# The last heads of a first attention in pairs of tiles, and the experts' routing in two halves under them

## The chip, the cores and the metric

The kernel runs on one core of one Trainium2 chip. The metric is the device time of one execution in microseconds. Five engines work side by side, each through its own program in a fixed order: PE (TensorE), DVE (VectorE), ACT (ScalarE), POOL (GpSimd) and SP (SyncE, which here only starts transfers). They wait for each other through semaphores.

## The reference

The input is eight batches (`NB`) of 512 tokens with 256 features: 32 tiles (`NN`) of 128 tokens. Four blocks follow each other, with two residual additions:

```python
x = x + _L0_attn_ref(_L0_cond_ref(x, ...), ...)      # causal attention, 16 heads of 64; then attention over the heads of a token
x = x + _L0_ffn_ref(_L0_cond2_ref(x, ...), ...)      # 8 experts, top 2, plus a shared expert; then attention and 8 experts, top 1
```

The change touches the end of the first line and the start of the second. The end of the first line works on each token by itself, over its 16 heads of 16 features:

```python
q, k, v = ...                                        # (B, T, 16 heads, 16), k and v through a latent of 64
att = softmax(einsum('bthd,btgd->bthg', q, k) / 4)   # 16 x 16 scores in each token
out = einsum('bthg,btgd->bthd', att, v) @ Wout + bout
```

The start of the second line routes each token to two of eight experts, and adds a shared expert:

```python
scores = softmax((x @ wt.T + repeat(g @ wg.T)) / 2)
topk_w, topk_idx = top_k(scores, 2)
y = sum of the two experts' outputs, weighted + (leaky(x @ sw_gate) * (x @ sw_up)) @ sw_down
```

## The kernel before, in words

The program has five parts with a fence between each two (`meet`): SP waits until all transfers of the part have landed, and every engine waits until all five have arrived. Part 0 is the first attention with the heads of batches 0 to 6, part 1 the "tail" (the heads of batch 7, and the routing of the others), part 2 the experts in pairs of slots, part 3 the second attention, part 4 the last experts. The order of each part is a list of steps written out by hand, and each engine walks the same list and does its share of each step. So a step's place in the list sets its place on all five engines.

**Heads of batch 7.** Four tiles `t` of 128 tokens. `q2` and `kv2` project on PE (DVE and ACT copy out). `hs` and `hv` come in quarters `u`: a product of 128x1024 elements (`product`, on POOL or DVE, for batch 7 half of them on each), then a reduction on DVE (`product_sum`) in the next step. The products lie in a ring of three cells. `hs_soft`, `hs_sum`, `hv_end` are small DVE and ACT operations; `turn_o` and `x1` project back on PE, POOL adds the bias to the residual (loaded by SP in step `turn_o`) and DVE adds both into the tile of `e_x1`, which SP also writes to `x1_scratch` (`x_scratch` in the profile) in step `x1`.

**Routing.** For each batch `r_turn` transposes 512 tokens on PE in two halves (ACT copies each), `r_score` computes the logits, ACT copies them, `r_back` transposes them back. These wait for each other in turn. The tokens are routed in two lots: batches 0 to 6 (`LOT[0]`, 28 tiles) and batch 7 (`LOT[1]`, 4 tiles). For a lot, `r_lgc`, `r_soft`, `r_rank`, `r_cnt`, `r_oh` compute the softmax and each token's two experts on DVE, and `count` gives each token its slot: two matmuls on PE and a running sum on DVE. `scatter n` writes tile n's rows to their two slots in `xe_scratch` with two indirect transfers, issued by POOL. `slots` finds the expert of each pair of slots. Part 2 then gathers the slots from `xe_scratch` with indirect transfers from POOL (`fetch`).

**Shared expert.** Steps `shared i`, 0 to 17: gate and up projections (PE), two DVE operations one step later, and in each second step from 3 on the down projection of an earlier batch, which ACT copies and SP writes to `y_scratch`.

**The order before.** The list of part 1 takes a step of the heads and a step of the rest in turn (`order_tail`): the seven batches' routing stands beside tiles 0 and 1, the first scatters and shared steps beside tiles 2 and 3, the remaining scatters behind, and last `e_load`, in which ACT starts 24 loads of expert weights. Behind the fence, part 2 begins with batch 7's routing, shared steps 14 to 17, the last eight scatters and `slots`, then the experts. PE's transposes and logits of the routing use one bank (`rR`) in part 1.

Of the kernel before, what the change touches and what calls it, by code (L numbers as in the profile page):

```python
# [242 lines left out]

def head_steps(b):
    yield [("turn_h", b, 0)]
    yield [("turn_h", b, 1)]
    yield [("lat", b)]

    def front(t):
        yield [("q2", b, t)]  # L250
        yield [("kv2", b, t)]

    def middle(t):
        for u in range(4):
            yield [("hs", b, t, u)]
        yield [("hs_soft", b, t)]
        yield [("hs_sum", b, t)]
        for u in range(4):
            yield [("hv", b, t, u)]
        yield [("hv_end", b, t)]  # L260

    def back(t):
        yield [("turn_o", b, t)]
        yield []
        yield [("x1", b, t)]

    late = 3 if b < NB - 1 else 2
    for i in range(NT + late):
# [14 lines left out]
def order_one():  # L283
# [49 lines left out]
    return out, [y for part in head_steps(NB - 1) for y in part]  # L333
# [637 lines left out]
def order_early():


    out = [("r_init",)]
    for b in range(NB - 1):
        out += [("r_turn", b), ("r_score", b), ("r_back", b)]
    out += routes(0)
    for n in range(*LOT[0]):
        out.append(("scatter", n))
        if n % 2:  # L980
            out.append(("shared", n // 2))
    return out


def order_tail(heads_left):

    early, out, due = order_early(), [("e_weights",)], -6.0
    for x in heads_left:
        out.append(x)
        due += 1.0  # L990
        while early and due >= 1.0:
            due -= 1.0
            out.append(early.pop(0))
    return out + early + [("e_load",)]


def order_two():
    b = NB - 1
    out = [("r_last",), ("r_turn", b), ("r_score", b), ("r_back", b)]
    i = 2 * (NB - 1)  # L1000
    for x in routes(1):
        out.append(x)
        if i < 2 * NB + 2 and x[0] in ("r_soft", "r_rank", "r_cnt", "count"):
            out.append(("shared", i))
            i += 1
    out += [("scatter", n) for n in range(*LOT[1])] + [("slots",), ("mha_load",)]
    out += [("expert", j) for j in range(4)] + [("gate", 0), ("gate", 1), ("places", 0), ("places", 1)]
    return out + [("expert", j) for j in range(4, NS_E // 2 + 3)]


def setup_two(k, nc, ins):
    sb, low = Arena(nc, k.split, k.hi), Arena(nc, k.base + 17 * 1024, k.split)
    k.tail = order_tail(k.tail1)
# [43 lines left out]
    k.rR, k.rL, k.rG = Ring(k.bank[0:1]), Ring(k.bank[2:3]), Ring([k.bank[1], k.bank[3]])  # L1057
# [44 lines left out]


def tensor_two(k, pe, w, order):
    did, ident = k.c.did, k.ident
    for step, *key in order:
# [4 lines left out]
        elif step == "r_last":  # L1111
            k.rR.cells, k.rR.n = [k.bank[0], k.bank[4]], 0
            k.rD.cells, k.rD.n = [k.bank[7], k.bank[0]], 0
# [27 lines left out]
        elif step == "count":  # L1141
# [3 lines left out]
            mr, mt = [k.rG.take((x, g), at("c_exc", g, 0), at("c_exc", g, 1)) for x in ("rank", "total")]  # L1145
# [206 lines left out]
def count(k, dv, w, g):  # L1352
# [4 lines left out]
    mr, mt = [k.rG.of((x, g)).ap[:, 0:n * E8].rearrange("p (t x) -> p t x", x=E8) for x in ("rank", "total")]  # L1357
# [1179 lines left out]
```

## Time and profile before

| | |
|---|---|
| median of 3 runs | 2675.94 us (2673.14 to 2695.26) |
| profiled execution | 2696.61 us, span 2694.7 us |
| PE busy | 2216.2 us, 82% of the span |
| DVE, ACT, POOL busy | 1473.1, 1181.2, 976.3 us (55%, 44%, 36%) |
| mean granted TensorE clock | 0.901 of full speed |

The shares are means over the whole span. The stretch of interest is a tenth of it, from about 1158 us (heads of batch 7 begin) to 1425.7 us (PE's first transposes for the experts), and has to be read by itself: the timeline of each engine there gives, for each group of instructions, when it began, how long it took, and in brackets how long the engine stood before it and which engine and tile ended the wait. "issue" stands for a wait for nothing that the profile shows.

### The profile page before, as it was taken

The page shows a single profiled execution, that of the slowest core. Times are in us where ns is not written, and L with a number is a line of the kernel's source. Part 1 is how long each engine was busy: PE and PEld are TensorE (multiplying, and loading weights), DVE is VectorE, ACT ScalarE, POOL GpSimd, SP SyncE. Part 2 cuts the span into 40 slices and gives each one's busy share as a digit, 9 for nine tenths or more (in the row PEclk, how much of TensorE's full clock was granted, in tenths as well). Part 3 has the DMA queues.
Part 4 walks back from the last instruction along what each step waited for, and adds up shares of the span by engine and source line. Part 5 has one row for each costly group of instructions (what it writes and reads, how often), then busy time and mean ns, then how long its engine had stood idle before and what let it go on. Part 6 is the DMA issues. An engine that isn't in the chain of part 4 may idle for free.

```text
span 2694.7 us, 33460 instructions
## 1 busy us (share of the span) xinstructions
PE 2216.2 (82%) x11652; PEld 1170.7 (43%) x11652; DVE 1473.1 (55%) x3091; ACT 1181.2 (44%) x2748; POOL 976.3 (36%) x751
## 2 busy tenths in 40 slices
PE   3989898989898989855857949899999988844996
PEld 1545555545455545522436823233333322222764
DVE  2336767676767676746523436666666660231336
ACT  1756666666666666611112411455555443220221
POOL 0105647474738374822725421112221110213005
PEclk9999999999999999967978967999999995576998
DMA  6032212112100000020344431111111004152214
GB/s 223 10 108 74 75 64 83 64 67 84 51 22 5 14 5 13 8 77 22 109 128 138 149 94 40 32 44 42 56 42 36 26 11 128 54 160 82 63 58 129
DMA packets 160464, 181.18 MB, mean 67 GB/s; under 512 B 18666, under 2 KB 144874, under 8 KB 160043
## 3 DMA queue, kind: packets, MB, share of 16 engines
q1 hardware_dynamic: 78402, 73.43, 8.9%
q10 hardware_dynamic: 69224, 70.99, 7.9%
q0 software_dynamic: 12672, 34.62, 4.1%
q8 instruction: 95, 1.56, 0.2%
q14 instruction: 71, 0.57, 0.1%
HBM read 88.03 MB, written 86.77 MB: 65 GB/s over the span
## 4 chain that ended last, share of the span: by engine, by line
PE 61%; DVE 12%; POOL 10%; ACT 8%; issue 4%; ACTq 3%; DMA 2%; SPq 0%; DVEq 0%; POOLq 0%
PE ps L1789 11%; POOL prod L793 6%; ACT m_pt L1917 6%; PE ps L513 4%; PE ps L527 4%; PE ps L1800 3%; PE ps L538 3%; PE ps L552 3%; DVE pb L676 3%; PE ps L562 3%; PE ps L2109 3%; PE ps L2117 3%; PE ps L1755 2%; DVE sc L805 2%; PE ps L1195 2%
## 5 line engine op out<-in xcount | busy, mean ns | idle before, releaser
L1917 ACT ACTIVATE m_pt<-ps 128x1024 f32<-128x1024 f32 x256 | 262.2, 1024 | 347.1 <-PE ps L1789 347.1
L1854 DVE TENSOR_REDUCE m_mx<-ps 128x2 f32<-128x1024 f32 x256 | 312.5, 1224 | 183.9 <-PE ps L1773 182.9
L676 DVE CUSTOM_DVE_ANT_0 pb<-ps,bias,snl 128x128 f32<-128x128 f32 (+3 forms) x512 | 260.8, 547 | 257.0 <-PE ps L527 254.4
L793 POOL TENSOR_TENSOR prod<-qs,kvs 128x1024 f32<-128x1024 f32 x120 | 284.3, 2395 | 230.6 <-issue 130.7
L1789 PE MATMUL ps<-m_q,m_k 32*128 32x512 f32 x1024 | 318.5, 701 | 56.6 <-ACT m_pt L1917 48.9
L793 POOL TENSOR_TENSOR prod<-sc,kvs 128x1024 f32<-128x1024 f32 x120 | 278.7, 2348 | 110.0 <-ACT sc L911 101.2
L873 ACT ACTIVATE pb<-pb,mst 128x129 f32<-128x129 f32 (+3 forms) x512 | 283.5, 559 | 69.3 <-DVE mst L676 67.3
L1773 PE MATMUL ps<-m_k,m_q 32*128 32x512 f32 x1024 | 293.2, 673 | 5.2 <-DVE m_mx L1854 5.2
L884 ACT ACTIVATE ptb<-ps 128x512 f32<-128x512 f32 (+2 forms) x384 | 181.6, 491 | 151.2 <-PE ps L538 148.2
L538 PE MATMUL ps<-ident,pb 128*128 128x128 f32 x1280 | 188.7, 284 | 63.5 <-ACT rsb L860 62.7
L538 PEld LDWEIGHTS ps<-ident,pb 128*128 128x128 f32 x1280 | 143.0, 144 | 125.3 <-ACT rsb L860 68.2
L527 PE MATMUL ps<-kz,qT 64*128 64x128 f32 (+3 forms) x1024 | 186.2, 442 | 0.0
L805 DVE TENSOR_REDUCE sc<-prod 128x64 f32<-128x1024 f32 x128 | 152.5, 1211 | 46.1 <-POOL prod L793 45.6
L1789 PEld LDWEIGHTS ps<-m_q,m_k 32*128 32x128 f32 x1024 | 83.3, 198 | 205.2 <-ACT m_pt L1917 184.2
L1944 POOL DMA_INDIRECT m_yg<-ye_scratch,e_pos x64 | 63.2, 987 | 289.8 <-DVE m_x L1842 253.5
L552 PE MATMUL ps<-ptb,vt 128*64 128x512 f32 (+3 forms) x1024 | 158.3, 452 | 7.9 <-DVE xr L750 7.9
L805 DVE TENSOR_REDUCE ob<-prod 128x64 f32<-128x1024 f32 x128 | 152.6, 1210 | 18.7 <-POOL prod L793 18.6
L1800 PE MATMUL ps<-m_pt,m_va 128*32 128x512 f32 x1024 | 150.6, 664 | 0.0
L513 PE MATMUL ps<-xnT,w_wq 128*128 128x512 f32 x256 | 134.4, 651 | 0.9
L1954 POOL TENSOR_TENSOR m_lnrs<-m_lnve,mhalf 128x1 f32<-128x1 f32 x32 | 17.7, 552 | 290.6 <-DVE m_lnve L761 290.6
L562 PE MATMUL ps<-w_wo,oTT 128*128 128x256 f32 x512 | 122.5, 383 | 0.1
L552 PEld LDWEIGHTS ps<-ptb,vt 128*64 128x64 f32 x1024 | 71.0, 141 | 92.1 <-issue 81.5
(310 smaller groups left out, 3764.1 us busy)
## 6 DMA issues: line engine op xcount, KB each, us to landing
xe_scratch<-zt ACTq DMA_DIRECT2D x32, 1024.0 KB, 4.5
ye_scratch<-e_ys SPq DMA_DIRECT2D x36, 256.0 KB, 2.1
hw_w<-in_w ACTq DMA_DIRECT2D x16, 512.0 KB, 3.6
xs_scratch<-zt ACTq DMA_DIRECT2D x1, 4992.0 KB, 16.3
h_xs<-xs_scratch SPq DMA_DIRECT2D x39, 128.0 KB, 2.2
ys_scratch<-h_ys SPq DMA_DIRECT2D x39, 128.0 KB, 1.7
xin<-in_x SPq DMA_DIRECT2D x8, 512.0 KB, 3.6
bias<-in_fside ACTq DMA_DIRECT2D x8, 512.0 KB, 11.8
```

Of the source, the lines that this page charges most:

```text
L513: i = pe.matmul(m.ap, k.wq[:, c, p * P:(p + 1) * P], xn.ap[:, c, :], start=(c == 0), stop=(c == 1))
L527: pe.matmul(ms[j].ap[:, 0:n], q.ap[DH * j:DH * j + DH, t * P:(t + 1) * P], kz.ap[DH * j:DH * j + DH, 0:n], start=False, stop=True, tile_po ...
L538: i = pe.transpose(m.ap[:, j * P:(j + 1) * P], pb[:, SEG[t] + kt * P:SEG[t] + (kt + 1) * P], ident[:, :])
L552: i = pe.matmul(m.ap[DH * j:DH * j + DH, kt * P:S], v.ap[:, kt, :], pt.ap[:, KEYCOL[kt]:KEYCOL[kt + 1]], start=(kt == 0), stop=(kt == NT - ...
L676: dv.tensor_tensor_reduce(pb.ap[:, j, SEG[t]:SEG[t] + n], rS.of(("S", b, p, t, j)).ap[:, 0:n], k.bias[:, h, CAUSAL[t]:CAUSAL[t + 1]], -1.0 ...
L793: e.tensor_tensor(out, one, two, ALU.mult).then_inc(*k.c.did(*product_done(step, b, t, u)))
L805: dv.tensor_reduce(heads(dst.ap[:, :])[:, 4 * u:4 * u + 4, :], src, AX, ALU.add).then_inc(*k.c.did(step + "_r", b, t, u))
L873: ac.activation(part, part, ACT.Exp, bias=ms[:, 0, j, t:t + 1], scale=-1.0, accum_out=ms[:, 1, j, t:t + 1]).then_inc(*did("exp", b, p, t, j))
L1773: x = pe.matmul(m.ap[:, i, :], band(q.ap, j)[:, t * P:(t + 1) * P], band(kk.ap, j), start=True, stop=True, tile_position=(32 * j, 0))
L1789: x = pe.matmul(m.ap[:, i, :], band(kk.ap, j)[:, kt * P:(kt + 1) * P], band(q.ap, j), start=True, stop=True, tile_position=(32 * j, 0))
L1854: dv.tensor_reduce(x.ap[:, t, 64 * half:64 * half + 64].rearrange("p (i r) -> p i r", i=2)[:, :, 16], k.qS.of((b, g, t, half)).ap, AX, ALU ...
L1917: ac.activation(p.ap[:, 2 * half:2 * half + 2, :], k.qE.of((b, g, kt, half)).ap, ACT.Exp).then_inc(*did("m_exp", b, g, kt, half))
```

## The change

`order_tail` is written anew. The heads of batch 7 go two tiles at a time: tiles 0 and 1 step by step together (`one`), with the `r_turn`, `r_score`, `r_back` of batches 0 to 6 between, two of these steps after each step of the heads; then tiles 2 and 3 together (`two`), with lot 0's routing, counting and shared steps 0 to 5 between. Then come `e_load`, the end of tiles 2 and 3 with shared steps 6 to 8, the 28 scatters of lot 0, batch 7's routing with shared steps 9 to 13, the four scatters of lot 1, `slots`, and shared steps 14 to 17. All of this stands ahead of the fence; part 2 begins with `mha_load` (nine loads on ACT) and the experts. The weights are loaded by SP in place of ACT. The routing's ring has three banks in place of one, and the counting's two matmuls get banks of their own (`rC`). `head_front`, `head_middle` and `head_back` hold the steps of a tile as the functions inside `head_steps` did.

```diff
+def last_heads():
+
+
+    b = NB - 1
+    start = [[("turn_h", b, 0)], [("turn_h", b, 1)], [("lat", b)]]
+    start += [x for t in range(2) for x in head_front(b, t)]
+    one = list(weave((head_middle(b, 0), 11), (head_middle(b, 1), 11), (head_front(b, 2), 2))) + list(head_front(b, 3))
+    two = list(weave((head_middle(b, 2), 11), (head_middle(b, 3), 11), (head_back(b, 0), 3), (head_back(b, 1), 3)))
+    return start, one, two, list(weave((head_back(b, 2), 3), (head_back(b, 3), 3)))
...
-def order_early():
-
-
-    out = [("r_init",)]
-    for b in range(NB - 1):
-        out += [("r_turn", b), ("r_score", b), ("r_back", b)]
-    out += routes(0)
-    for n in range(*LOT[0]):
-        out.append(("scatter", n))
-        if n % 2:
-            out.append(("shared", n // 2))
-    return out
-
-
-def order_tail(heads_left):
-
-    early, out, due = order_early(), [("e_weights",)], -6.0
-    for x in heads_left:
-        out.append(x)
-        due += 1.0
-        while early and due >= 1.0:
-            due -= 1.0
-            out.append(early.pop(0))
-    return out + early + [("e_load",)]
-
-
-def order_two():
-    b = NB - 1
-    out = [("r_last",), ("r_turn", b), ("r_score", b), ("r_back", b)]
-    i = 2 * (NB - 1)
-    for x in routes(1):
-        out.append(x)
-        if i < 2 * NB + 2 and x[0] in ("r_soft", "r_rank", "r_cnt", "count"):
+def order_tail():
+
+
+    start, one, two, end = last_heads()
+    turns = [("r_init",)] + [(x, b) for b in range(NB - 1) for x in ("r_turn", "r_score", "r_back")]
+    out = [("e_weights",)] + [x for part in start for x in part]
+    for part in one:
+        out += part + turns[:2]
+        turns = turns[2:]
+    out += turns
+    chain, i = routes(0), 0
+    for n, part in enumerate(two):
+        out += part + chain[:1]
+        chain = chain[1:]
+        if n % 2 == 0:
             out.append(("shared", i))
             i += 1
-    out += [("scatter", n) for n in range(*LOT[1])] + [("slots",), ("mha_load",)]
-    out += [("expert", j) for j in range(4)] + [("gate", 0), ("gate", 1), ("places", 0), ("places", 1)]
+    out += chain + [("e_load",)]
+    for part in end:
+        out += part + [("shared", i)]
+        i += 1
+    out += [("scatter", n) for n in range(*LOT[0])]
+    b = NB - 1
+    for x in [("r_turn", b), ("r_score", b), ("r_back", b)] + routes(1):
+        out.append(x)
+        if x[0] in ("r_turn", "r_back", "r_soft", "r_rank", "r_cnt"):
+            out.append(("shared", i))
+            i += 1
+    return out + [("scatter", n) for n in range(*LOT[1])] + [("slots",)] + [("shared", j) for j in range(i, 2 * NB + 2)]
+
+
+def order_two():
+    out = [("mha_load",)] + [("expert", j) for j in range(4)] + [("gate", 0), ("gate", 1), ("places", 0), ("places", 1)]
     return out + [("expert", j) for j in range(4, NS_E // 2 + 3)]
...
-    k.rR, k.rL, k.rG = Ring(k.bank[0:1]), Ring(k.bank[2:3]), Ring([k.bank[1], k.bank[3]])
+    k.rR, k.rL, k.rG = Ring([k.bank[0], k.bank[5], k.bank[6]]), Ring(k.bank[2:3]), Ring([k.bank[1], k.bank[3]])
+    k.rC = Ring([k.bank[2], k.bank[0]])
...
+        if step == "e_load":
+            for x in range(E8):
+                g4 = k.gu[:, x, :].rearrange("p (c k m) -> p c k m", c=2, k=2)
+                sp.dma_start(g4[:, :, 0, :], ins["moe_gate"][x].rearrange("(c p) m -> p c m", p=P)).then_inc(*did("d_gu", 2 * x))
+                sp.dma_start(g4[:, :, 1, :], ins["moe_up"][x].rearrange("(c p) m -> p c m", p=P)).then_inc(*did("d_gu", 2 * x + 1))
+                sp.dma_start(k.dn[:, x, :], ins["moe_down"][x]).then_inc(*did("d_dn", x))
...
-            mr, mt = [k.rG.take((x, g), at("c_exc", g, 0), at("c_exc", g, 1)) for x in ("rank", "total")]
+            mr, mt = [k.rC.take((x, g), at("c_exc", g, 0), at("c_exc", g, 1)) for x in ("rank", "total")]
...
-                load("gu", 2 * x, g4[:, :, 0, :], ins["moe_gate"][x].rearrange("(c p) m -> p c m", p=P))
-                load("gu", 2 * x + 1, g4[:, :, 1, :], ins["moe_up"][x].rearrange("(c p) m -> p c m", p=P))
-                load("dn", x, k.dn[:, x, :], ins["moe_down"][x])
```

POOL, from the heads' products of batch 7 to the first gather (`prod` the products, `xr` the residual, `xe_scratch` the scatters, `e_xs` the gathers). Before:

```order
L793 TENSOR_TENSOR prod<-sc_116,kvs_114 128x1024 x2
L793 TENSOR_TENSOR prod<-qs_109,kvs_112 128x1024
L1584 DMA xe_scratch<-e_x_144,e_sposi 32768x256 x4
L952 TENSOR_TENSOR xr_125<-xr_125,w_bout 128x256
L793 TENSOR_TENSOR prod<-qs_109,kvs_112 128x1024
L1584 DMA xe_scratch<-e_x_144,e_sposi 32768x256 x6
...
L1584 DMA xe_scratch<-e_x_144,e_sposi 32768x256 x4
L952 TENSOR_TENSOR xr_125<-xr_125,w_bout 128x256
L1584 DMA xe_scratch<-e_x_144,e_sposi 32768x256 x28
L1593 DMA e_xs_182<-xe_scratch,e_gix 128x256 x2
```

Now:

```order
L805 TENSOR_TENSOR prod<-sc_115,kvs_112 128x1024
L805 TENSOR_TENSOR prod<-sc_116,kvs_113 128x1024
L805 TENSOR_TENSOR prod<-sc_115,kvs_112 128x1024
L805 TENSOR_TENSOR prod<-sc_116,kvs_113 128x1024
L964 TENSOR_TENSOR xr_124<-xr_124,w_bout 128x256
L964 TENSOR_TENSOR xr_125<-xr_125,w_bout 128x256
L1591 DMA xe_scratch<-e_x_144,e_sposi 32768x256 x64
L1600 DMA e_xs_182<-xe_scratch,e_gix 128x256 x2
```

The scatters stood between the products of tiles 2 and 3; now all 64 stand behind the last product and the last residual of the heads.

SP, from the residual loads of tiles 0 and 1 to the experts' first write (`xr` the residual, `x_scratch` the heads' output, `e_y` the shared expert's). The 24 loads of the weights stand in the middle, of which the first three are shown. Before:

```order
L465 DMA x_scratch<-e_x_144 128x256
L461 DMA xr_125<-in_x 128x256
L465 DMA x_scratch<-e_x_144 128x256
L1094 DMA y_scratch<-e_y_179 128x4x256
L461 DMA xr_124<-in_x 128x256
L1094 DMA y_scratch<-e_y_180 128x4x256
L1094 DMA y_scratch<-e_y_179 128x4x256
L465 DMA x_scratch<-e_x_144 128x256
L461 DMA xr_125<-in_x 128x256
L465 DMA x_scratch<-e_x_144 128x256
```

Now:

```order
L1109 DMA y_scratch<-e_y_179 128x4x256
L477 DMA x_scratch<-e_x_144 128x256 x2
L1109 DMA y_scratch<-e_y_180 128x4x256
L1101 DMA ew_gu<-in_moe_gate 128x2x128
L1102 DMA ew_gu<-in_moe_up 128x2x128
L1103 DMA ew_dn<-in_moe_down 128x256
...
L1103 DMA ew_dn<-in_moe_down 128x256
L473 DMA xr_124<-in_x 128x256
L473 DMA xr_125<-in_x 128x256
L1109 DMA y_scratch<-e_y_179 128x4x256
L477 DMA x_scratch<-e_x_144 128x256 x2
```

The residual loads of tiles 2 and 3 stand behind the 24 weight loads, which before were ACT's.

PE, from the first projections of batch 7's heads on (`hT` the input, `latT` the latent, `e_x` the rows that are routed). Before:

```order
L599 MATMUL ps<-w_awq,hT 128x256 x2
L605 MATMUL ps<-w_wup,latT 128x512
L1110 MATMUL ps<-ew_cT,ew_wg 8x8
L1120 MATMUL ps<-ident,e_x_144 128x128 x8
L1127 MATMUL ps<-e_xT,ew_wt 8x512 x2
L1139 MATMUL ps<-ident,e_lgT_198 128x8 x4
L599 MATMUL ps<-w_awq,hT 128x256 x2
L1120 MATMUL ps<-ident,e_x_144 128x128 x8
```

Now:

```order
L611 MATMUL ps<-w_awq,hT 128x256 x2
L617 MATMUL ps<-w_wup,latT 128x512
L611 MATMUL ps<-w_awq,hT 128x256 x2
L617 MATMUL ps<-w_wup,latT 128x512
L1125 MATMUL ps<-ew_cT,ew_wg 8x8
L1132 MATMUL ps<-ident,e_x_144 128x128 x8
L1139 MATMUL ps<-e_xT,ew_wt 8x512 x2
...
L1151 MATMUL ps<-ident,e_lgT_198 128x8 x4
L611 MATMUL ps<-w_awq,hT 128x256 x2
L1132 MATMUL ps<-ident,e_x_144 128x128 x8
```

Tile 1's two projections stand ahead of the routing, and tile 2's first behind the third batch of it.

## Rows read from the trace of the kernel before

**Rows 1.** Windows of core 0: stretch, length, busy PE, PEld, DVE, ACT, POOL, clock, DMA.

```profile
1158.00:1237.50 79.50, 47.43 (x144) 17.64 (x142) 37.13 (x41) 18.34 (x35) 21.22 (x10) 0.71 0.18 59
1237.50:1364.50 127.00, 88.27 (x236) 46.87 (x236) 72.57 (x95) 17.85 (x34) 79.63 (x67) 0.85 0.25 86
1380.60:1425.70 45.10, 22.85 (x69) 12.66 (x69) 15.83 (x49) 5.69 (x10) 10.89 (x12) 0.69 0.30 99
```

**Rows 2.** Timeline of POOL: start, length, instruction, wait before it and its releaser.

```profile
1264.11 1.21 POOL L1584 DMA_INDIRECT xe_scratch<-e_x,e_sposi  x1 [24.31 <-DVE e_sposi L1388]
...
1321.00 1.73 POOL L1584 DMA_INDIRECT xe_scratch<-e_x,e_sposi  x1 [0.30 <-issue]
...
1343.73 0.97 POOL L1584 DMA_INDIRECT xe_scratch<-e_x,e_sposi  x1 [2.12 <-issue]
...
1360.21 0.96 POOL L1584 DMA_INDIRECT xe_scratch<-e_x,e_sposi  x1 [0.31 <-issue]
...
1406.28 0.98 POOL L1584 DMA_INDIRECT xe_scratch<-e_x,e_sposi  x1 [45.12 <-DVE e_sposi L1388]
...
1415.16 0.96 POOL L1584 DMA_INDIRECT xe_scratch<-e_x,e_sposi  x1 [0.30 <-issue]
...
1421.60 0.99 POOL L1593 DMA_INDIRECT e_xs<-xe_scratch,e_gix  x1 [5.48 <-DMA xe_scratch<-e_x,e_sposi]
```

**Rows 3.** Timeline of PE, the same columns.

```profile
1179.26 0.63 PE L1120 MATMUL ps<-ident,e_x 128*128 128x128 f32 x4 [0.95 <-ACT e_cs L1518]
...
1222.58 1.88 PE L1127 MATMUL ps<-e_xT,ew_wt 128*8 128x512 f32 x4 [0.69 <-ACT e_xT L1523]
...
1380.64 1.97 PE L1120 MATMUL ps<-ident,e_x 128*128 128x128 f32 x8 [16.23 <-SPq L2441]
...
1425.68 1.12 PE L1184 MATMUL ps<-ident,e_xs 128*128 128x128 f32 x4 [19.61 <-DMA e_xs<-xe_scratch,e_gix]
```

**Rows 4.** Groups of PE by line, 1156 to 1420.5: busy, mean ns, idle before.

```profile
L1127 PE MATMUL ps<-e_xT,ew_wt 128*8 128x512 f32 x32 | 25.4, 943 | 5.5 <-ACT e_xT L1523 5.5
...
L1120 PE MATMUL ps<-ident,e_x 128*128 128x128 f32 x64 | 12.7, 337 | 23.6 <-SPq L2441 16.2 <-ACT e_xT L1523 6.4 <-ACT e_cs L1518 1.0
...
L599 PE MATMUL ps<-w_awq,hT 128*128 128x256 f32 x16 | 5.4, 466 | 0.0
...
L1139 PE MATMUL ps<-ident,e_lgT 8*128 8x8 f32 x32 | 3.6, 218 | 5.1 <-ACT e_lgT L1528 5.1
```

**Rows 5.** Groups of DVE by line, 1156 to 1380: busy, mean ns, idle before.

```profile
L805 DVE TENSOR_REDUCE ob<-prod 128x64 f32<-128x1024 f32 x16 | 19.3, 1212 | 14.0 <-POOL prod L793 13.9
...
L793 DVE TENSOR_TENSOR prod<-qs,kvs 128x1024 f32<-128x1024 f32 x8 | 12.4, 1550 | 8.2 <-ACT kvs L905 8.2
...
L793 DVE TENSOR_TENSOR prod<-sc,kvs 128x1024 f32<-128x1024 f32 x8 | 10.7, 1336 | 0.0
...
L1330 DVE TENSOR_TENSOR e_aT<-ps,e_lk 128x512 f32<-128x512 f32 x13 | 9.0, 692 | 6.7 <-PE ps L1170 6.4
```

**Rows 6.** Timeline of DVE.

```profile
1183.30 2.20 DVE L793 TENSOR_TENSOR prod<-qs,kvs 128x1024 f32<-128x1024 f32 x1
...
1233.27 0.39 DVE L1292 COPY e_lg<-ps 128x224 f32<-128x224 f32 x1 [3.22 <-PE ps L1139]
...
1251.78 0.27 DVE L1485 TENSOR_SCALAR e_oh<-e_gt 128x224 f32<-128x224 f32 x1
...
1255.49 0.62 DVE L1360 COPY e_cum<-ps 128x448 f32<-128x448 f32 x1 [2.31 <-PE ps L1149]
```

**Rows 7.** Timeline of ACT and its queue (ACTq).

```profile
1364.45 0.39 ACTq L1492 DMA_DIRECT2D ew_gu<-in_moe_gate  x1
...
1411.65 0.51 ACTq L1492 DMA_DIRECT2D m_x<-y_scratch  x1
```

**Rows 8.** Chain that ended last, in order of time: start, length, what.

```profile
1376.85 3.47 DMA ew_dn<-in_moe_down
```

**Rows 9.** Transfers by line, 1290 to 1430: issuer, count, KB, us to landing.

```profile
xr<-in_x SPq DMA_DIRECT2D x2, 128.0 KB, 2.8
```

More of the change, by code:

```diff
@@ L241, in pre_steps, with head_front, head_middle, head_back @@
     yield [("vals", b)]
+def head_front(b, t):
+    yield [("q2", b, t)]
+    yield [("kv2", b, t)]
+def head_middle(b, t):
+    for u in range(4):
+        yield [("hs", b, t, u)]
+    yield [("hs_soft", b, t)]
+    yield [("hs_sum", b, t)]
+    for u in range(4):
+        yield [("hv", b, t, u)]
+    yield [("hv_end", b, t)]
+def head_back(b, t):
+    yield [("turn_o", b, t)]
+    yield []
+    yield [("x1", b, t)]
 def head_steps(b):
@@ L247, in head_steps @@
     yield [("lat", b)]
[L249 to L268, printed above, removed]
+    for i in range(NT + 3):
         parts = []
-        if i >= late:
-            parts.append((back(i - late), 3))
+        if i >= 3:
+            parts.append((head_back(b, i - 3), 3))
         if i < NT:
-            parts.append((front(i), 2))
+            parts.append((head_front(b, i), 2))
         if 1 <= i <= NT:
-            parts.append((middle(i - 1), 11))
+            parts.append((head_middle(b, i - 1), 11))
         yield from weave(*parts)
+def last_heads():
[5 more added lines that the diff above has]
+    return start, one, two, list(weave((head_back(b, 2), 3), (head_back(b, 3), 3)))
 CLEARS = 32
@@ L332, in order_one @@
     out += [y for part in hd[0] for y in part]
-    return out, [y for part in head_steps(NB - 1) for y in part]
+    return out, [y for stage in last_heads() for part in stage for y in part]
 def setup_one(k, nc, ins):
@@ L1012, in setup_two @@
     sb, low = Arena(nc, k.split, k.hi), Arena(nc, k.base + 17 * 1024, k.split)
-    k.tail = order_tail(k.tail1)
+    k.tail = order_tail()
     k.exc, k.inc = [None, None], [None, None]
@@ L1086, in sync_two @@
 def sync_two(k, sp, w, order):
-    did = k.c.did
+    did, ins = k.c.did, k.ins
     for step, *key in order:
-        if step == "shared":
+        if step == "e_load":
[4 more added lines that the diff above has]
+                sp.dma_start(k.dn[:, x, :], ins["moe_down"][x]).then_inc(*did("d_dn", x))
+        elif step == "shared":
             i = key[0]
@@ L1110, in tensor_two @@
             pe.matmul(m.ap[0:E8, 0:NB], k.wg[:, :], k.cT[:, :], start=True, stop=True).then_inc(*did("e_cs", 0))
-        elif step == "r_last":
-            k.rR.cells, k.rR.n = [k.bank[0], k.bank[4]], 0
-            k.rD.cells, k.rD.n = [k.bank[7], k.bank[0]], 0
         elif step == "r_turn":
@@ L1172, in tensor_two @@
         elif step == "mha_load":
+            k.rR.cells, k.rR.n = [k.bank[0], k.bank[4]], 0
             k.rD.cells, k.rD.n = [k.bank[7], k.bank[2]], 0
@@ L1356, in count @@
     n = 2 * (n1 - n0)
-    mr, mt = [k.rG.of((x, g)).ap[:, 0:n * E8].rearrange("p (t x) -> p t x", x=E8) for x in ("rank", "total")]
+    mr, mt = [k.rC.of((x, g)).ap[:, 0:n * E8].rearrange("p (t x) -> p t x", x=E8) for x in ("rank", "total")]
     w.wait_ge(at("c_mm", g, 1))
```

3 lines of the change are left out of this document (removed).

## The prediction

> **What bounds the kernel now.** I read the stretches of time first, then the timeline of each engine in the one stretch that the change touches. The first attention ends near 1158 us, the paired experts' first transposes start at 1425.68 [rows 3]. The change moves work only between these two marks; before and behind them the programs are the same. In that stretch no engine is full: PE, DVE and POOL are each busy for half of the time or less from 1158 to 1237.5, and POOL alone comes over 60% from 1237.5 to 1364.5 [rows 1]. So what counts is the chain. On POOL it reads like this [rows 2]: the first scatter at 1264.11 waited for the slot numbers from DVE; 56 scatters then run to 1361.2, mixed with POOL's products for the last two tiles of heads; POOL idles 45 us until 1406.28, because batch 7's routing stands behind the fence; 8 more scatters, a wait for their landing, the first gather at 1421.60, and PE 4.1 us later. A run of scatters with nothing between costs 1.27 us each (1343.73 to 1360.21 is 13 steps). Ahead of the fence ACT issues 24 weight loads from 1364.45 [rows 7] on; the last is issued at 1376.85 (to about 1377.3) and lands at 1380.32 [rows 8], and PE resumes at 1380.64 [rows 3], 0.3 us later.
>
> **What goes.** The fence now stands behind all 64 scatters, so the hole of 45 us on POOL goes, and so do the 16 us in which nothing computes while ACT issues the weights. In return no scatter may start until the last head tile is out, since all of them stand behind POOL's last two additions of the residual. The question is when that is.
>
> **First half of the heads.** Its length is set by the routing chain of seven batches on PE and ACT, not by the heads. The first routing transpose is at 1179.26 [rows 3]; tile 1's two projections and their copies now come first, about 1.3 us (bounds 0.5 and 2.5), so 1180.6. A batch is eight transposes (12.7/8 = 1.59), a wait for ACT (5.5/8 = 0.69), the scores (25.4/8 = 3.18), a wait (5.1/8 = 0.64) and the transposes back (3.6/8 = 0.45) [rows 4]: 6.55, and 45.9 for seven. Before it took 54 (1179.26 to 1233.27, when DVE copies the logits [rows 6]), mainly since one bank made the second transposes wait for the first copy; now there are three banks. Three more projections stand in the chain, 1.35 each (5.4/4) or less: 3.5 in all. Half one ends at 1230. DVE needs some 34.5 us for two tiles (below), has one wait for tile 2's projection, which stands behind the third batch, and is done by about 1221: hidden under the chain, by 9 us.
>
> **Second half.** Here DVE is the bound. All its work in the first two stretches is 37.13 + 72.57 = 109.7 us [rows 1]. Of that, 13 shared steps take twice 9.0 = 18.0 [rows 5] (two operations each, of one size), or 1.38 a step. Routing of seven batches is 14.4: from 1233.27 to 1252.05 [rows 6] less five head operations between, 4.4 (three of 1.2 and two of 0.4). The counting runs from 1255.49 to 1263.8 [rows 6], 8.3. The counting ends where POOL's first scatter begins, at 1264.11, less 0.3. The rest, 69, is four tiles of heads, so 34.5 for two. Half two holds two tiles (34.5), routing (14.4), counting (8.3) and four shared steps (5.5): 62.7. PE's two counting matmuls took 3.4 us between the one-hots and the first copy [rows 6]; 2.7 us of other DVE work now stands there, so 0.7 of wait. Tiles 0 and 1 are out at 1230 + 63.4, about 1294.
>
> **Then SyncE.** It writes two tiles, and then issues the 24 weight loads ahead of the residual rows of tiles 2 and 3: 28 issues. ACT needed 1364.45 to 1377.3 for its 24, 12.9 us or 0.54 each [rows 7, 8]; I take the same for SyncE, 15.0 (bounds 12 and 17). A residual load takes 2.8 to land [rows 9], the last weights took 3.5 from the start of their issue [rows 8]; beside them I take 3.3. POOL's addition is 0.7. This is a wait the change creates: POOL has no product left from about 1291 on and stands until 1294 + 15.0 + 3.3 + 0.7 = 1313.0. The weights' issue is still not hidden; it has moved from ahead of the fence to ahead of the scatters.
>
> **Scatters.** 64 at 1.27 are 81.2. The 56 of before have two pauses in which nothing is waited for that the profile shows, one of 2.12 [rows 2] and one like it; less the usual 0.3 each, about 3.7. End at 1397.9. Under them lie batch 7's routing and shared steps 8 to 17 on PE, DVE and ACT. In the stretch from 1237.5 to 1364.5 PE was busy for 88.27 us [rows 1], with fourteen shared steps and some head work, so a step costs at most 6.3 and ten at most 63; batch 7's routing adds a batch's 6.55. That is 70, inside 85: hidden, but it would be the next bound.
>
> **Behind the scatters.** From the last scatter's end to the first gather 5.2 us (1416.4 to 1421.60), now with a fence of 0.3 between, and 4.1 from there to PE [rows 2, 3]: PE at 1407.5. What is new is that ACT issues its nine attention loads before the first copy; they took about 6 us, the last of them at 1411.65 [rows 7]; the first stood right behind ACT's last copy, so ACT is free about 0.8 after PE's first transposes, and the gathers share the DMA engines with these loads. I take 1.5 (bounds 0.5 and 5). That makes 1409.0, 16.7 before 1425.7. Phase two has about ten hand-overs between engines that each work in a fixed order, and I have costed one at 0.7; the others I bound by 0 and 12 us and take 3, nearer to nothing, because most of the partners are over half idle. **Sum: 14 us gained.**
>
> The expert stage itself stays: PE sets its pace, and it starts from a rest either way.
>
> **Rivals.** *The lock.* Two tiles at once put DVE's products beside POOL's more often. A DVE product beside one of POOL took 2.20 us [rows 6], while the means are 1.55 and 1.34 [rows 5]. Were all eight in half two at 2.20, that is 4 x 0.65 + 4 x 0.86 = 6 us more; with the hand-overs at their upper bound (9 more than I took) the gain is gone: 2676. It decides when DVE's half two passes 80 us. For it: three product cells serve two tiles. Against: the more numerous reductions show no such growth, 1.21 each in the mean [rows 5]. The Trainium skill, SBUF — State Buffer, section Who interferes with whom, says that a DVE instruction with two SBUF inputs and a GpSimd one that reads SBUF exclude each other for a whole instruction; by that rule each of the eight waits for a POOL product, and the trace agrees in the slowed row.
>
> *A quicker chain.* The scores took 1.88 us in one batch [rows 3] against a mean of 3.18: PE ran at the higher of its two levels there. Half one packs PE more densely (three banks), and if all seven batches ran so, 9 us more would be gained: 23, or 2653. Against: the granted clock over this stretch is 0.71 [rows 1], and the chain still waits at every step.
>
> *Slower.* 64 scatters now stand in one row, and anything that slows their issue counts 64 times. Beside a DVE product a scatter took 1.73 us [rows 2] in place of 0.96; were that the rule for all that DVE does now beside the scatters (shared steps, batch 7's routing), 64 x 0.77 = 49 us are added, and the result is 35 us slower, 2711. It decides from 0.65 us per scatter for a slowdown of 1%. Against it: the products are over by then, and 14 scatters in a row beside DVE's shared steps kept 1.27 [rows 2], as did the eight beside the counting and `slots` (1406.28 to 1415.16 is seven steps of 1.27). The Trainium skill, SBUF — State Buffer, section SBUF: two separate sides, warns that descriptors of a GpSimd DMA can't be written while DVE runs a mode with two ports; by that, DVE's copies beside the scatters could do it too.
>
> *The change doesn't do it.* If the weights' issue and the residual's late load eat what the fence gives, little is left; this is in the sum already (about 20 us of standing POOL), and an issue of 17 us with 5 of landing and 5 behind the scatters leaves 7: inside my range.
>
> **Numbers.** The profiled execution took 2696.61 (span 2694.7); the median of the runs is 2675.94 and they spread from 2673.14 to 2695.26. The sum of -14 is made against the profile's own time, which becomes 2682.6; I apply the same to the median: **2662**. Chances: this forecast, 6 to 20 us gained, 0.62; the quicker chain 0.14; gain gone (between 6 gained and 10 lost) 0.19; slower by more than that 0.05. A measurement of this kernel can tell about 1%, 27 us, from no change. Over that on the quick side lies only the outer part of the quicker chain, with every other bound at its best: 0.08. Slower by over 1%: 0.04. Within: 0.88. The range: 17 us to the quick side and 18 to the slow one takes in the bounds of the sum (issue 3, hand-overs 9, gathers 4, lock 6 against 9 of clock) and a few us of the spread of runs: 2645 to 2680.
>
> **What would show it.** In the profile after: the last transposes back of batch 6 near 1230 (if at 1222, the quicker chain); tile 1's output on DVE near 1294 to 1300 (over 1310: lock and hand-overs); POOL idle for some 20 us ahead of the first scatter, released by the DMA of the residual, and that scatter near 1313 to 1316; 64 scatters at 1.27 with two or three pauses (at over 1.9: the slow rival); first gather about 5.5 us behind them; the experts' first transposes near 1409 to 1414. I am wrong if half one waits for DVE rather than for PE's chain, if the weights take far from 13 us to issue on SyncE, or if shared steps outlast the scatters.

## The result, and the profile after

The changed kernel took 2663.61 us in the median of 20 runs (2649.49 to 2676.92), the kernel before 2680.34 in as many (2671.78 to 2700.17). The ratio is 0.9933, with a 95% interval of 0.9911 to 0.9955: 18 us less (12 to 24), which is inside 1% and inside the range forecast (2645 to 2680; 2662 was the likeliest). The profiled execution of the changed kernel has a span of 2653.1 us, 41.6 less than the one of before. Some 19 us of that difference aren't the change's, as run e5 below shows; so I compare **the part that the change touches**, from PE's transposes of `hn` (the end of the first attention, 1156.28 before and 1156.80 now) to PE's first transposes for the experts. It was 269.4 us long (to 1425.68 [rows 3]) and is 247.0 now (to 1403.85).

The stretches of the changed kernel, as in [rows 1] (length, busy time and instructions of PE, PEld, DVE, ACT and POOL, the granted clock, the DMA share, GB/s): half one, half two, POOL's wait for the residual, the scatters, the fence and first gather.

```profile
1158.00:1222.00 64.00, 36.23 (x146) 16.97 (x145) 37.07 (x40) 17.66 (x33) 22.76 (x9) 0.82 0.25 77
1222.00:1286.00 64.00, 39.70 (x95) 20.88 (x94) 62.02 (x78) 7.93 (x16) 23.05 (x9) 0.76 0.03 9
1286.00:1305.40 19.40, 16.78 (x55) 9.62 (x53) 4.35 (x8) 4.13 (x8) 1.40 (x2) 1.00 0.81 243
1305.40:1394.30 88.90, 52.21 (x156) 29.38 (x156) 24.36 (x62) 12.14 (x21) 62.19 (x64) 0.82 0.36 126
1394.30:1403.80 9.50, 0.00 (x0) 0.00 (x0) 0.00 (x0) 0.00 (x0) 5.29 (x7) 0.50 0.71 209
```

Each stretch has another limit: DVE is full in the second (62 of 64), in the third POOL stands and SyncE issues, in the fourth POOL alone sets the pace. POOL's timeline (start, length, instruction, idle time before it and what ended it) answers to [rows 2]:

```profile
1272.97 5.56 POOL L805 TENSOR_TENSOR prod<-sc,kvs 128x1024 f32<-128x1024 f32 x2 [14.05 <-DVE ob L817]
1303.89 1.40 POOL L964 TENSOR_TENSOR xr<-xr,w_bout 128x256 f32<-128x256 f32 x2 [25.36 <-DMA xr<-in_x]
1305.48 1.21 POOL L1591 DMA_INDIRECT xe_scratch<-e_x,e_sposi  x1 [0.19 <-issue]
...
1325.48 0.97 POOL L1591 DMA_INDIRECT xe_scratch<-e_x,e_sposi  x1 [2.35 <-issue]
1326.76 0.96 POOL L1591 DMA_INDIRECT xe_scratch<-e_x,e_sposi  x1 [0.30 <-issue]
...
1345.20 0.97 POOL L1591 DMA_INDIRECT xe_scratch<-e_x,e_sposi  x1 [2.11 <-issue]
...
1384.51 0.98 POOL L1591 DMA_INDIRECT xe_scratch<-e_x,e_sposi  x1 [2.11 <-issue]
...
1393.37 0.96 POOL L1591 DMA_INDIRECT xe_scratch<-e_x,e_sposi  x1 [0.30 <-issue]
1397.02 1.00 POOL L1600 DMA_INDIRECT e_xs<-xe_scratch,e_gix  x1 [2.69 <-POOLq L2448]
```

The hole of 45 us is gone. A wait of 25.4 us for the residual's rows stands ahead of the scatters in its place, and the row of scatters has four pauses (2.35, 2.11, 2.10 and 2.11 us, one after each 14). SyncE's queue shows why the rows came late: two tile writes, 24 weight loads, then the rows (22 of the loads, between the first and the last, are left out).

```profile
1285.66 0.80 SPq L477 DMA_DIRECT2D x_scratch<-e_x  x2
1287.26 0.37 SPq L1109 DMA_DIRECT2D y_scratch<-e_y  x1
1287.67 0.51 SPq L1101 DMA_DIRECT2D ew_gu<-in_moe_gate  x1
...
1299.82 0.47 SPq L1103 DMA_DIRECT2D ew_dn<-in_moe_down  x1
1300.34 0.90 SPq L473 DMA_DIRECT2D xr<-in_x  x2
```

PE in half one (the routing's chain) and at the end; [rows 3, 4] are those of before:

```profile
1205.83 1.09 PE L1132 MATMUL ps<-ident,e_x 128*128 128x128 f32 x8
1207.66 1.88 PE L1139 MATMUL ps<-e_xT,ew_wt 128*8 128x512 f32 x4 [0.74 <-ACT e_xT L1530]
1210.31 0.41 PE L1151 MATMUL ps<-ident,e_lgT 8*128 8x8 f32 x4 [0.77 <-ACT e_lgT L1535]
1210.65 1.09 PE L1132 MATMUL ps<-ident,e_x 128*128 128x128 f32 x8
...
1220.35 1.13 PE L611 MATMUL ps<-w_awq,hT 128*128 128x256 f32 x4
...
1371.78 1.99 PE L1182 MATMUL ps<-ew_sd,e_aT 128*128 128x256 f32 x8 [0.69 <-ACT e_y L1552]
1403.85 1.08 PE L1197 MATMUL ps<-ident,e_xs 128*128 128x128 f32 x4 [30.07 <-DMA e_xs<-xe_scratch,e_gix]
```

A batch of routing takes 4.82 us (1205.83 to 1210.65), 7.7 before (54 for seven [rows 3, 6]). The last shared step ends at 1373.8, 20 us ahead of the scatters: hidden, as forecast.

### The profile page after: what moved, and what is told of

The parts are those of the page before. It is cut to its first block, busy times and chain, and to the rows that moved or that the text cites. A ratio compares the mean times of both kernels' runs of the same rounds, so it can differ in the third digit from the quotient of the medians.

```text
span 2653.1 us, 33457 instructions
## 1 busy us (share of the span) xinstructions
PE 2178.8 (82%) x11652; PEld 1162.1 (44%) x11652; DVE 1475.3 (56%) x3091; ACT 1180.5 (44%) x2748; POOL 976.6 (37%) x751
## 4 chain that ended last, share of the span: by engine, by line
PE 59%; DVE 12%; POOL 10%; ACT 8%; issue 5%; ACTq 3%; DMA 2%; SPq 1%; POOLq 0%; DVEq 0%
PE ps L1796 11%; ACT m_pt L1924 6%; POOL prod L805 5%; PE ps L525 4%; PE ps L539 4%; PE ps L550 3%; PE ps L564 3%; DVE sc L817 3%; PE ps L1807 3%; DVE pb L688 3%; PE ps L574 3%; PE ps L2116 3%; PE ps L2124 3%; PE ps L1762 3%; PE ps L1208 2%
## 5 line engine op out<-in xcount | busy, mean ns | idle before, releaser
L1796 PE MATMUL ps<-m_q,m_k 32*128 32x512 f32 x1024 | 307.5, 678 | 57.5 <-ACT m_pt L1924 49.4
L550 PE MATMUL ps<-ident,pb 128*128 128x128 f32 x1280 | 188.6, 284 | 63.4 <-ACT rsb L872 62.7
L817 DVE TENSOR_REDUCE sc<-prod 128x64 f32<-128x1024 f32 x128 | 152.2, 1209 | 32.9 <-POOL prod L805 32.6
```

Of the source, the lines that this page charges most:

```text
L550: i = pe.transpose(m.ap[:, j * P:(j + 1) * P], pb[:, SEG[t] + kt * P:SEG[t] + (kt + 1) * P], ident[:, :])
L817: dv.tensor_reduce(heads(dst.ap[:, :])[:, 4 * u:4 * u + 4, :], src, AX, ALU.add).then_inc(*k.c.did(step + "_r", b, t, u))
L1796: x = pe.matmul(m.ap[:, i, :], band(kk.ap, j)[:, kt * P:(kt + 1) * P], band(q.ap, j), start=True, stop=True, tile_position=(32 * j, 0))
```

## The experiments

All are compared with the kernel before on the same chip. "Part" is the part named above, in the one profiled execution of each; it is cut at POOL's first scatter (A) and at the end of its last (B), C is what follows to the experts. The last column is the second attention behind the experts, from PE's first transposes of `m_x` to POOL's next scatter, whose code is the same in all of them. The changed kernel and e5 are the same program, and their parts differ by 4.1 us, A by 1.3, B by 1.7 and C by 1.1: differences of that size in a single profile tell nothing.

| kernel | ratio (95%) | part | A | B | C | 2nd attention, clock |
|---|---|---|---|---|---|---|
| before | 1 | 269.4 | | | | 843.3, 0.87 |
| changed | 0.9933 (0.9911 to 0.9955) | 247.0 | 148.7 | 88.9 | 9.5 | 825.2, 0.89 |
| e5, changed again | 0.9932 (0.9902 to 0.9962) | 251.1 | 150.0 | 90.5 | 10.6 | 834.6, 0.88 |
| e2, weights on SyncE only | 0.9969 (0.9943 to 0.9995) | 260.0 | | | | 839.2, 0.88 |
| e4, batch 7 behind the fence | 1.0021 (0.9994 to 1.0048) | 275.2 | 150.4 | | | 827.2, 0.89 |
| e3, 28 scatters fewer | 0.9855 (0.9819 to 0.989) | 234.1 | 150.1 | 60.3 | 23.8 | 821.4, 0.90 |
| e1, rows first | 0.9874 (0.9839 to 0.991) | 239.4 | 135.6 | 91.3 | 12.5 | 825.3, 0.89 |
| e6, and 10 scatters early | 0.9881 (0.9849 to 0.9913) | 224.7 | 121.8 | 92.9 | 10.0 | 821.7, 0.90 |
| e7, one tile at a time | 0.9965 (0.9939 to 0.9991) | 254.1 | 155.3 | 88.6 | 10.3 | 821.5, 0.90 |
| e8, one bank | 0.9987 (0.9964 to 1.0009) | 260.2 | 161.4 | 88.4 | 10.4 | 838.5, 0.88 |
| e9, chain's steps ahead | 0.994 (0.9912 to 0.9969) | 250.9 | 151.5 | 89.7 | 9.7 | 834.7, 0.88 |
| e10, loads late | 0.9918 (0.989 to 0.9947) | 244.3 | 148.5 | 89.1 | 6.8 | 833.6, 0.88 |
| e11, e6 + e9 + e10 | 0.9828 (0.9794 to 0.9862) | 224.9 | 123.7 | 94.4 | 6.8 | 845.2, 0.87 |
| e12, and 4 more early | 0.9867 (0.9829 to 0.9904) | 220.4 | 111.4 | 98.4 | 10.7 | 839.0, 0.88 |

**e5: how much of the profile's difference is the change's.**

> The changed kernel once more, unchanged, as the reference for its neighbours on this chip. If the profile's 42 us between the two kernels were the change's, its time behind the first attention (from the experts' first transposes to the end, 1249 us in the one profile and 1269 in the other) would be 1249 again and the ratio near 0.985; if that part is the spread of runs, the ratio stays near 0.993 and the part behind varies.

The ratio stayed at 0.9932, and the part behind the experts' first transposes was 1258.7 us long, neither 1249 nor 1269. The rows of the second attention (columns as above) of before, the changed kernel, e6 and e11 say what differs:

```profile
1574.30:2417.60 843.30, 730.78 (x3972) 250.55 (x3972) 453.81 (x685) 341.96 (x394) 140.35 (x182) 0.87 0.19 58
```
```profile
1554.40:2379.60 825.20, 711.96 (x3972) 245.74 (x3972) 453.85 (x685) 341.85 (x394) 140.41 (x184) 0.89 0.19 59
```
```profile
1531.50:2353.20 821.70, 707.69 (x3972) 244.71 (x3972) 453.93 (x685) 341.98 (x394) 140.33 (x183) 0.90 0.20 59
```
```profile
1536.80:2382.00 845.20, 732.03 (x3972) 250.80 (x3972) 453.92 (x685) 341.78 (x394) 140.23 (x184) 0.87 0.19 58
```

The same 3972 matmuls, and DVE and ACT busy alike to 0.2 us; only PE's busy time and the granted clock move, and the stretch with them, by 24 us. It doesn't follow the change: e11 is the slowest and has the changed kernel's order. So the part (22.4 us less in one profile, 18.3 in the other) and the ratio (18) agree, and the profiles' further 19 us are this spread.

**e2: one half of the change alone.** SyncE's step from the change, put into the kernel before, behind the last head step:

```
-    return out + early + [("e_load",)]
+    return out + [("e_load",)] + early
```

> The kernel before with one part of the change alone: SyncE, not ACT, issues the 24 weight loads, behind the last head tile's write, under the scatters. Theory (the 16 us in which ACT issues and all others stand are a cost by themselves): about 15 us less than before, 2665, which is all that the whole change gave, while POOL's hole for batch 7's routing stays at some 28 us. Rival (the issue is hidden anyway, or the loads slow the scatters): within 4 us of before.

The part is 9.4 us shorter and the ratio 8 us (1 to 15), not 15, though the ratio's interval just reaches 15: the shared steps and the landing of their last write now held the fence up, and PE resumed at 1373.69 in place of 1380.64 [rows 3]; POOL's hole was 33.6 us. In that profile PE also stood 4.65 us ahead of the last down projection for a copy of ACT's, which itself stood 5.1 us for something that the profile doesn't name. So in this profile 9 of the weights' 16 us were there to be had without the rest of the change.

**e4: the other half taken back.** The rows of the order for batch 7 (`r_turn`, `r_score`, `r_back`, `routes(1)`, its scatters) stand in `order_two` again, and with them `slots`, the last shared steps and, behind them, `mha_load`.

> The changed kernel with batch 7's routing and its 8 scatters put back behind the fence. Theory (the hole behind the fence is what the change takes away): POOL stands some 26 us between the 56 scatters and the 8, and the kernel takes about 2690, more than the kernel before. Rival (the gain comes from the quicker chain and the weights, and the hole was worth little): 2665 to 2672.

28 us longer than the changed kernel in the part (24 against e5), and as slow as before:

```profile
1388.80 0.96 POOL L1593 DMA_INDIRECT xe_scratch<-e_x,e_sposi  x1 [0.30 <-issue]
1422.21 0.97 POOL L1593 DMA_INDIRECT xe_scratch<-e_x,e_sposi  x1 [32.46 <-DVE e_sposi L1403]
```

With the order of the heads, the three banks and SyncE's loads all in place, the gain is gone. It is the hole (32.5 us here) that pays, and the late first scatter is its price.

**e3: what bounds the row.** `for u in range(2)` becomes `for u in (range(1, 2) if n < LOT[0][1] else range(2))`; so 28 rows of scatters aren't written.

> The changed kernel without 28 of the 64 scatters (the first slot's row of each token tile of batches 0 to 6 isn't written). Theory (the scatters' row sets the end, the shared steps are next, which ended on PE at 1373.8): POOL's row is 28 x 1.27 + 4 shorter, but only some 19 us show, about 2645. Rival (POOL isn't what the fence waits for): no gain. Second rival (nothing else is near): all 40 us.

B fell by 29 to 30, the part by 13 to 17. POOL's waits in that stretch (who waited for whom: us in total, times, the longest):

```profile
POOL e_xs L1600 <- SPq L2448: 16.5, 1, 16.5
POOL xe_scratch L1591 <- DVE e_sposi L1401: 11.8, 1, 11.8
```

The shared steps and batch 7's routing are next, some 13 to 17 us below the scatters, as the first theory had it.

**e1 and e6: the wait ahead of the scatters.** e1 moves `("e_load",)` behind the loop over `end`. e6 adds:

```
-    out += chain
+    out += chain + [("scatter", n) for n in range(5)]
```

> SyncE issues the residual rows of tiles 2 and 3 ahead of its 24 weight loads. Theory (POOL's 25.4 us of standing ahead of the scatters are SyncE's queue): the rows are issued about 12.6 us sooner, the first scatter comes some 20 us behind the last product in place of 32, everything behind it moves by 12 to 13 us, and the kernel takes about 2651. Rival (the shared steps or the weights' landing are the next bound at once): under 5 us gained.

> As e1, and POOL issues the first 10 scatters before its two additions for tiles 2 and 3. Theory (POOL's row sets the end): the row starts some 14 us earlier, and 12 us come on top of e1's gain. Rival (behind e1 the shared steps are the bound, as its trace shows, where the last of them ended at 1387.6, after the scatters): within 3 us of e1, with POOL idle ahead of the first gather for over 10 us.

A is 13.1 us shorter in e1 (14.4 against e5), what the queue was said to cost. In its profile only 7.6 of it reached the experts: the shared steps ended last, at 1387.7 (the scatters had ended at 1386.1). PE was at the lower clock for several of them, and PE and ACT also stood for things that the profile doesn't name: PE 4.91 us ahead of 1368.15, ACT 7.87 ahead of 1356.86. What held them isn't known. It isn't the order on PE, since e6 has the same one, and there the shared steps ended at 1367.9 and the scatters set the end. e6's rival, that nothing is left beyond e1, fell in the profiles: POOL stood 2.7 us ahead of the first gather, not over 10, and the part is 14.7 us shorter still, and 22.3 to 26.4 shorter than the changed kernel's. The whole kernel's times don't confirm the further gain: e1 is 1.3% under before and e6 1.2%, on two chips, so it stands on one profile of each. e6 shows too what a scatter costs beside DVE's products; DVE, then POOL:

```profile
1279.02 1.22 DVE L805 TENSOR_TENSOR prod<-sc,kvs 128x1024 f32<-128x1024 f32 x1
1281.29 1.22 DVE L805 TENSOR_TENSOR prod<-sc,kvs 128x1024 f32<-128x1024 f32 x1
```

```profile
1279.11 2.21 POOL L1592 DMA_INDIRECT xe_scratch<-e_x,e_sposi  x1 [0.19 <-issue]
1281.62 1.72 POOL L1592 DMA_INDIRECT xe_scratch<-e_x,e_sposi  x1 [0.31 <-issue]
1283.65 0.96 POOL L1592 DMA_INDIRECT xe_scratch<-e_x,e_sposi  x1 [0.30 <-issue]
```

**e7: what the pairs are worth.** Each half runs its tiles one behind the other, with one step of the chain behind each part (and a shared step behind each fourth, not each second); the edit of half one:

```
-    one = list(weave((head_middle(b, 0), 11), (head_middle(b, 1), 11), (head_front(b, 2), 2))) + list(head_front(b, 3))
+    one = list(weave((head_middle(b, 0), 11), (head_front(b, 2), 2))) + list(weave((head_middle(b, 1), 11), (head_front(b, 3), 2)))
```

> The changed kernel with the last heads one tile at a time inside its two halves (tile 0, then 1, with the routing's chain; tile 2, then 3, with its end), all else kept. Theory (a pair fills DVE's waits for POOL's products and ACT's exponentials): DVE reaches tile 1's output 5 to 10 us later than with pairs, and the kernel is as much slower. Rival (the pair pays for DVE and POOL standing in each other's way as much as it fills): within 3 us.

A is 5.3 us longer, the part 3.0, both against e5 on the same chip, and tile 1's output came 6.0 later (counted from `hn`), as the theory had it; but 3.0 is less than the 4.1 between the changed kernel and e5, the ratios' intervals overlap, and PE's scores took 3.8 us more in this profile at the lower clock. Two tiles at a time are no loss, and worth 5 us at most; that they are worth anything isn't shown.

**e8: what the banks are worth.** `Ring([k.bank[0], k.bank[5], k.bank[6]])` becomes `Ring(k.bank[0:1])`.

> The changed kernel with one PSUM bank for the routing's transposes and scores in place of three. Theory (the banks made the chain quick: a batch took 4.8 us in the changed kernel and 7.7 before): half one is 10 to 14 us longer, and 8 to 14 of it reach the end of the kernel. Rival (the chain is quick because PE ran at its higher clock there): a batch takes 5 to 6 us with one bank, and the kernel changes by under 5.

Tile 3's projection, which ends half one, reached DVE 77.2 us behind `hn`, in e5 66.8: 10.4 longer, and 9.1 of it reached the experts. With one bank a batch reads

```profile
1212.78 1.88 PE L1139 MATMUL ps<-e_xT,ew_wt 128*8 128x512 f32 x4 [0.69 <-ACT e_xT L1530]
1215.44 0.41 PE L1151 MATMUL ps<-ident,e_lgT 8*128 8x8 f32 x4 [0.77 <-ACT e_lgT L1535]
1215.78 0.66 PE L1132 MATMUL ps<-ident,e_x 128*128 128x128 f32 x4
1217.12 0.66 PE L1132 MATMUL ps<-ident,e_x 128*128 128x128 f32 x4 [0.69 <-ACT e_xT L1530]
1218.46 3.19 PE L1139 MATMUL ps<-e_xT,ew_wt 128*8 128x512 f32 x4 [0.69 <-ACT e_xT L1530]
```

5.7 us from scores to scores at the higher clock (4.8 with three banks), and in the next batch the scores take 3.19. So one bank adds 0.9 us of waiting a batch, 6 in all. But the stall of 5.67 us that e9 is about isn't in e8, and so PE's waits in the chain sum to 14.4 us, against 14.8 in e5. The chain is 8.5 us longer by PE's own time: it was busy for 21.5 us with the scores of the seven batches, in e5 for 13.3. Both theories had a part. Why the scores ran at the lower clock isn't settled. Fewer gaps in PE's work don't explain it: e11, with three banks and only 9.9 us of waits in the chain, had three of its seven scores at 3.2 to 3.5 us, one of them here:

```profile
1190.96 3.53 PE L1140 MATMUL ps<-e_xT,ew_wt 128*8 128x512 f32 x4 [0.74 <-ACT e_xT L1531]
```

No run holds the gaps and changes the clock alone.

**e9: the one stall in half one.** In the changed kernel ACT's exponentials stood ahead of a routing copy, and PE waited 5.67 us for it at 1198.13. `out += part + turns[:2]` becomes `out += turns[:2] + part`.

> The changed kernel with two steps of the routing's chain ahead of, not behind, each part of half one's heads. Theory (half one is the chain plus one stall of 5 us, in which ACT's exponentials stood ahead of a routing copy): the stall goes or halves, half one ends 3 to 5 us earlier, and the kernel gains as much. Rival (the stall moves to the next batch, or DVE's own work for two tiles is the bound): under 1.5 us.

No gain. The stall moved to the next batch's copies, as the rival said; ACT in e9, then PE:

```profile
1199.65 0.42 ACT L923 ACTIVATE sc<-sc 128x256 f32<-128x256 f32 x1 [2.71 <-DVE sc L744]
1199.97 1.06 ACT L1530 ACTIVATE e_xT<-ps 128x512 f32<-128x512 f32 x2
```
```profile
1201.09 3.58 PE L1139 MATMUL ps<-e_xT,ew_wt 128*8 128x512 f32 x4 [3.82 <-ACT e_xT L1530]
```

**e10, e11, e12: the loads, and all together.** e10 moves ACT's nine loads behind `("expert", 2)`; e11 is e6 with e9's and e10's edits; e12 puts scatters 0 and 1 of e11's first five behind part 7 of `two`.

> The changed kernel with ACT's nine loads for the second attention behind the paired experts' third step, not ahead of the first. Theory (the first gathers share the DMA engines with these loads: 6.8 and 7.9 us from the first gather to PE in two profiles, 4.1 before): this time is 4.1 to 4.5 us again, 3 us gained. Rival (the gathers are slow for another reason, or ACT's issues now hold up its first copies for 4.6 us): no gain.

> e6, e9 and e10 together. Theory (three separate terms of one chain): e6's time less 4 less 3, about 36 us under the changed kernel in the part from the first attention's last transposes to the experts, which is some 218 us long. Rival (the shared steps take the end over once the scatters start early enough): no better than e6 less 3.

> As e11, and four of the scatters stand ahead of POOL's last two products, in the 14 us in which POOL waited there. Theory: they start when the slots are known, 5 us ahead of the products, and shorten the row behind by as much, less 1 or 2 for scatters beside DVE's products: 3 to 4 us under e11. Rival (a scatter that is slowed holds up the product that DVE waits for): 0 or a loss.

From the first gather to PE's transposes it is 4.09 us in e10, and within 0.05 of that in e11 and e12; in all kernels with `mha_load` right behind the fence it is 6.6 to 7.9. In before, e2 and e4, where the nine loads had been issued 9 us or more ahead of the first gather, it is 4.1 too. PE in e10 (the first gather began at 1403.34):

```profile
1407.43 1.09 PE L1197 MATMUL ps<-ident,e_xs 128*128 128x128 f32 x4 [27.41 <-DMA e_xs<-xe_scratch,e_gix]
```

C fell by 2.7 (3.8 against e5), as expected. e11 is not better than e6 in the part: its C is 3.2 shorter, A and B are 3.4 longer, and e9's edit, which gains nothing, is in it. e12's scatters start 12.3 us earlier, but the row is 4 longer (POOL's last two products, 4.66 us, stand in it), and then the shared steps' last write held the fence (C is 10.7): 4.5 gained in the part, which the ratio (0.9867) doesn't bear out. Of all kernels run e11 has the lowest median, 2636.04 us, 1.7% under before (1.4 to 2.1); its interval overlaps e12's.

## Why the prediction held, step by step

The mechanism was right and the gain larger than forecast: 22 us in one profile, 18 in the other and 18 by the ratio, in place of 14. The first scatter came at 1305.5, not at 1313 to 1316, and PE at 1403.9, not at 1409 to 1414. That the forecast of 2662 lies within 2 us of 2663.61 is luck: the kernel before has a median of 2680.34 in 20 runs, 4.4 over the 2675.94 in three from which I subtracted, and that offsets the 3 to 4 us that I forecast too little.

**The limit and the exchange** were right: the hole of 45 us and the weights' 16 went, a late first scatter came. e4 shows that the hole carries the gain, e2 that of the weights' 16 us on ACT 9 could be had alone.

**Half one** was the step that was mis-sized: 1230 forecast, DVE's next projection at 1221.5, which is the mark (1222) that the quicker-chain rival had named. The batches took 4.82 in place of 6.55, mostly because the scores took 1.88, not the mean of 3.18 [rows 4]. I had argued against it from the granted clock of [rows 1] (0.71), as if it would stay; it is 0.82 now, and e8 shows that one bank brings most of the slow scores back, though not why. One stall of 5.67 us behind ACT's exponentials, 4.9 more than the usual wait there, which I didn't have, gave part back.

**Half two** was right in the sum, 63.4 forecast for DVE and 63.7 measured (1221.5 to 1285.2), but not in its terms. The heads took 32.6 us, not 34.5, since none of DVE's products was slowed: 1.21 or 1.22 each. The routing took 16.7, not 14.4, because the lock between DVE and POOL, which I had looked for in the products, fell on it:

```profile
1243.13 3.24 DVE L1490 TENSOR_TENSOR e_cmp<-e_cmp,ew_before 128x1792 f32<-128x1792 f32 x1
1246.40 2.43 DVE L1492 TENSOR_TENSOR e_cmp<-e_cmp 128x1792 f32<-128x1792 f32 x1
```

Before, the same two took 2.02 and 2.03. POOL had a product until 1244.49 and then the additions for tiles 0 and 1, which took 4.97 us (those for tiles 2 and 3 took 1.40, at 1303.89). The two errors cancel.

**SyncE's queue** was right to 1.3 us: 19.0 forecast from tile 1 to the first scatter, 20.3 measured; the 24 loads took 12.6 us, and e1 gave 13 of it back.

**The row of scatters** was 4 us short: two pauses were read from before, where one of POOL's products (behind 28 scatters) hid the third and the hole (behind 56) the fourth; there is one after each 14 scatters in the changed kernel. The slower rival fell: 1.27 per scatter beside DVE's shared steps and routing, but for two of the 64 that took 1.09 and 1.25.

**Behind the scatters** two errors offset each other in part: 2.7 to the first gather, not 5.5, and 6.8 from there to PE, not 5.6. (The last scatter of before ended at 1416.1, not at 1416.4 as the prediction has it; its 5.2 should be 5.5 without the fence.) The 1.5 for the loads were really 2.7 to 3.8 (e10). The 3 us for hand-overs weren't needed. Why the first gather came at 2.7 in most of the kernels, and at 5.5 in before but at 2.2 in e4, which waited for the same landing, isn't settled; where it was late in e1 and e12, the last write of the shared steps held the fence (SyncE waited 2.1 us for its landing in both).

In sum 8.5 us more were gained in half one and 1.6 behind the scatters, 4 lost in them and 1.6 ahead of them, and the allowance of 3 was free: 7.5 on top of the 14 forecast. Measured are 22 in one profile, 18 in the other, and 18 by the ratio.

## What to carry to other kernels

A hole on one engine is worth what the work that takes its place costs, so look at what the engine waits for next: here it was a queue that issued 24 loads nobody needed yet ahead of two that everybody waited for. Put the loads with a waiting reader first in a queue, and those with none last. When the profiles of two kernels differ by more than their medians do, compare a stretch whose code is the same, with its instruction counts and granted clock, before the change is credited with it.

## What the hardware showed that I had not expected

- **The clock of an unchanged stretch.** The second attention, same 3972 matmuls, took 821 to 845 us in fourteen profiles, with the granted clock between 0.90 and 0.87. One profile of each kernel could not have shown 18 us in the whole time; two medians of 20 runs did.
- **A pause after each 14 scatters.** Four of 2.1 to 2.35 us in a row of 64 (0.3 is usual), of which two were visible before. In all fourteen profiles no gap behind a 14th, 28th, 42nd or 56th scatter is under 2.1 us; mostly it is 2.1, and the longest that no named wait explains is 4.6 (e1). Why isn't shown. POOL's own work fits into it: in e12 the two additions of 1.42 us stand there, and from the 14th scatter to the 15th it is 2.11 all the same.
- **A scatter beside DVE's products.** 1.72 and 2.21 us in e6, in place of 0.96. It is a wait for the end of DVE's operation, and no lower pace: the product of 1281.29 ends at 1282.51, the scatter beside it at 1283.34, 0.83 us later. In the fourteen profiles 34 scatters took between 1.08 and 2.22 us beside a DVE operation with both inputs in SBUF that had begun before them (five of 1.73 or 1.74 in before, one of which is in [rows 2]); 32 of them ended 0.82 to 0.89 us behind its end, and two that led the row 1.08. Seven that began beside such an operation of under 0.5 us weren't held. Beside reductions, and beside the shared steps' operations, which have one input in PSUM, scatters kept 0.96 to 1.02. The Trainium skill, SBUF — State Buffer, section Who interferes with whom, infers that a `tensor_tensor` of two SBUF inputs takes only the read interface, which descriptors don't need. This case's rows disagree. A scatter reads its slot numbers from SBUF; whether that is what waits, no run shows.
- **Gathers beside other loads.** The first gather took 6.6 to 7.9 us to reach PE with nine loads on ACT's queue beside it and 4.0 to 4.1 without.
